# First attention: steps placed anew between the heads, and the normalised x written by ScalarE

## What is computed

```python
x = L0_attn_x                      # (32, 256, 128): 32 batches of 256 tokens of 128
xn = _layernorm(x, axis=-1)        # (x - mean) / sqrt(var + 1e-5)
x = x + _L0_attn_ref(xn, Wq, Wk, Wv, Wo) + _L0_ffn_ref(xn, ...)

# _L0_attn_ref: 16 heads of width D = 8
q, k, v = split_heads(xn @ Wq), split_heads(xn @ Wk), split_heads(xn @ Wv)
qc, kc = q - mean(q), k - mean(k)
cov = einsum('bhsd,bhtd->bhst', qc, kc) / D
scores = cov + q_var[..., :, None] * k_var[..., None, :] / D   # variances with ddof=1
out = einsum('bhst,bhtd->bhsd', softmax(scores), v)
return out.transpose(0, 2, 1, 3).reshape(b, s, e) @ Wo
```

## Time and profile before

| | us |
|---|---|
| median of 3 runs | 1303.16 |
| lowest, highest | 1302.62, 1307.37 |
| the profiled execution | 1305.62 |
| its span | 1304.0 |
| TensorE busy (matmul) | 1059.3 |
| VectorE busy | 780.4 |
| GpSimd busy | 704.3 |
| ScalarE busy | 677.1 |
| mean granted clock of TensorE | 0.838 of 2.4 GHz |

### The profile page before, as it was taken

How to read it: one execution, slowest core, us unless ns; L and a number is a source line. 1 busy time by engine, 2 the same in 40 slices (tenths; PEclk the granted TensorE clock), 3 DMA queues, 4 the chain that set the end, 5 groups by cost and what they waited for, 6 DMA issues and landing times.

```text
span 1304.0 us, 35270 instructions
## 1 busy us (share of the span) xinstructions
PE 1059.3 (81%) x12261; PEld 635.2 (49%) x12278; DVE 780.4 (60%) x2112; ACT 677.1 (52%) x1315; POOL 704.3 (54%) x1078
## 2 busy tenths in 40 slices
PE   1378878878888724999988988989888989889887
PEld 0345546555655512788844444444444444444443
DVE  3557667676675642333367667666677666766662
ACT  2155665665566211444436566556666555555565
POOL 3125565566556464222246677566686565765661
PEclk9978777777777755999969799878989877898799
DMA  7232212212212127777611111111111111111110
GB/s 153 31 99 50 48 52 63 47 47 61 54 42 51 41 35 164 219 224 221 193 41 39 31 37 39 33 29 33 41 35 36 33 29 33 37 33 33 26 43 26
DMA packets 135621, 84.23 MB, mean 65 GB/s; under 512 B 39936, under 2 KB 122752, under 8 KB 135552
## 3 DMA queue, kind: packets, MB, share of 16 engines
q1 hardware_dynamic: 124160, 55.98, 17.1%
q0 software_dynamic: 11392, 27.35, 8.1%
HBM read 49.02 MB, written 33.73 MB: 63 GB/s over the span
## 4 chain that ended last, share of the span: by engine, by line
PE 63%; ACT 11%; DVE 10%; issue 9%; SPq 3%; DMA 2%; POOL 0%; ACTq 0%; DVEq 0%; POOLq 0%
PE bank L678 53%; DVE rowmin L1144 4%; PE bank L716 3%; PE bank L772 2%; ACT Vexp L1577 2%; PE bank L956 1%; ACT oT L1490 1%; ACT h2s L1615 1%; ACT prob L1584 1%; ACT gxh L1592 1%; PE bank L778 1%; PE bank L688 1%; ACT gxb L1598 1%; DVE rsum L1162 1%; ACT oT_all L1509 1%
## 5 line engine op out<-in xcount | busy, mean ns | idle before, releaser
L1531 ACT ACTIVATE prob<-bank 128x512 f32<-128x512 f32 x512 | 302.9, 599 | 248.3 <-PE bank L678 242.7
L1144 DVE TENSOR_REDUCE rowmin<-bank 128x2 f32<-128x512 f32 x512 | 329.7, 685 | 99.0 <-PE bank L678 98.9
L678 PE MATMUL bank<-QKT 32*128 32x256 f16 x2048 | 218.6, 296 | 54.9 <-DVE rowmin L1144 50.7
L678 PE MATMUL bank<-prob,V 128*25 128x256 f32 x2048 | 157.1, 430 | 0.7 <-ACT prob L1531 0.7
L678 PEld LDWEIGHTS bank<-QKT 32*128 32x128 f16 x2048 | 63.7, 95 | 192.4 <-DVE rowmin L1144 85.2
L558 POOL DMA_INDIRECT token_rows<-rows,spots x128 | 127.6, 997 | 36.8 <-issue 36.8
L604 POOL DMA_INDIRECT xa<-expert_out,place x128 | 125.9, 984 | 39.3 <-issue 29.7
L502 POOL TENSOR_TENSOR sq<-feat 128x512 f32<-128x512 f32 x32 | 33.2, 1039 | 151.5 <-ACT feat L1502 151.5
L1666 ACT ACTIVATE hmid<-bank,wrow,up_scale 128x512 f32<-128x512 f32 x80 | 57.9, 773 | 95.0 <-PE bank L678 95.0
L678 PE MATMUL bank<-hnT,in_wT 128*128 128x512 f32 x64 | 59.8, 1033 | 52.5 <-ACT hnT L1546 36.4
L618 POOL DMA_DIRECT2D expert_out<-y x40 | 30.2, 754 | 122.3 <-DVE y L1420 118.7
(11 more groups left out here) (223 smaller groups left out, 2062.6 us busy)
## 6 DMA issues: line engine op xcount, KB each, us to landing
xrow<-token_rows SPq DMA_DIRECT2D x40, 258.0 KB, 3.2
wrow<-weight_rows SPq DMA_DIRECT2D x40, 257.0 KB, 3.4
expert_out<-y POOLq DMA_DIRECT2D x40, 256.0 KB, 3.0
token_rows<-xrow SPq DMA_DIRECT2D x16, 258.0 KB, 6.6
xg<-in_L_attn_x SPq DMA_DIRECT2D x64, 64.0 KB, 1.9
x_in<-in_L_attn_x SPq DMA_DIRECT2D x32, 128.0 KB, 2.3
xa<-in_L_attn_x SPq DMA_DIRECT2D x64, 64.0 KB, 2.0
out_base<-acc SPq DMA_DIRECT2D x64, 64.0 KB, 1.7
```

Of the source, the lines that this page charges most:

```text
L678: return pe.matmul(o, l, r, start=start, stop=stop, skip_group_check=True)
L1144: dve.tensor_reduce(rowmin[h // 8][:, :, h % TILE_ROWS, h // TILE_ROWS % HALF], row_scores[i % 3][:].rearrange("p (s t) -> p s t", s=ST), ...
L1531: act.activation(prob[:, h % 8].rearrange("p t s -> p (t s)"), col_scores[h % 2][:], ACT.Exp, scale=exp_register).then_inc(s_exp, 1)
```

## The change

The tables get new numbers: on all three engines the pieces stand at other heads, so that the groups of probability x V come at heads 2, 6, 11 and 15 instead of 1, 5, 9 and 13, and two pieces often share a head. VectorE does `split_shift(1)` and the statistics before the head's row maximum instead of behind it, and out, half0 and half1 stand at another distance from TensorE's. The normalised x is no longer written by GpSimd: VectorE makes var + eps and -mean (two operations of two columns), GpSimd makes rstd and -mean x rstd of them, and ScalarE writes xn with two ACTIVATEs (Identity, with scale and bias per partition) at head 5.

```diff
--- before.py
+++ after.py
@@ -40,10 +40,10 @@
 
 
 LEAD = 4
-PE_AT = dict(half1=0, out=3, merge=6, half0=8, project=11, v=2, shift0=7, x=10, qk=12, shift1=15)
-DVE_AT = dict(half1=0, out=2, shift0=4, half0=7, shift1=12, statistics=1)
-ACT_AT = dict(shift1=0, copy_out=2, v=3, merged=7, shift0=8, x=10, output=12, features=13)
-PE_PV = (5, 9, 13, 1)
+PE_AT = dict(half1=0, out=5, merge=7, half0=9, project=13, v=3, shift0=5, x=7, qk=9, shift1=13)
+DVE_AT = dict(half1=1, out=5, half0=10, statistics=0, shift1=12, shift0=3)
+ACT_AT = dict(shift1=0, copy_out=2, v=3, normalise=5, shift0=6, merged=7, x=7, features=9, output=14)
+PE_PV = (6, 11, 15, 2)
 
 
 
@@ -203,6 +203,9 @@
         stats = sb("stats", [P, ST, 6])
         mv = sb("mv", [P, ST, 2])
         rstd = sb("rstd", [P, ST])
+        var_x = sb("var_x", [P, ST])
+        minus_mean = sb("minus_mean", [P, ST])
+        centre = sb("centre", [P, ST])
         minus_half = sb("minus_half", [P, 2 * TILES])
         epsilon = sb("epsilon", [P, TILES])
         xn = sb("xn", [P, ST, E])
@@ -356,6 +359,7 @@
         s_x = [sem(f"s_x{p}") for p in range(2)]
 
         s_var = sem("s_var")
+        s_rstd = sem("s_rstd")
         s_xn = sem("s_xn")
         s_xt_ps = sem("s_xt_ps")
         s_xt = sem("s_xt")
@@ -478,18 +482,13 @@
                 pool.tensor_tensor(gain_root[:], gain[:], minus_half[:, 0:1], ALU.pow)
                 pool.tensor_tensor(var_scale[:], exp_scale[:], halves[:, 0:1], ALU.pow).then_inc(s_gain_root, 1)
 
-            def normalise_x(n, p):
+            def scale_x(n):
                 pool.wait_ge(s_var, n + 1)
                 if positive(n):
-                    pool.wait_ge(s_xt_ps, n)
-                pool.tensor_tensor(rstd[:], mv[:, :, 1], epsilon[:, 0:ST], ALU.add).then_inc(s_pool, 1)
+                    pool.wait_ge(s_xn, n)
+                pool.tensor_tensor(rstd[:], var_x[:], minus_half[:, 0:ST], ALU.pow).then_inc(s_pool, 1)
                 pool.wait_ge(s_pool, own.next())
-                pool.tensor_tensor(rstd[:], rstd[:], minus_half[:, 0:ST], ALU.pow).then_inc(s_pool, 1)
-                pool.wait_ge(s_pool, own.next())
-                for st in range(ST):
-                    ins = pool.tensor_scalar(xn[:, st, :], x_in[p][:, st, :], mv[:, st, 0:1],
-                                             rstd[:, st:st + 1], ALU.subtract, ALU.mult)
-                ins.then_inc(s_xn, 1)
+                pool.tensor_tensor(centre[:], minus_mean[:], rstd[:], ALU.mult).then_inc(s_rstd, 1)
 
             def features_stack(n, p):
 
@@ -623,7 +622,7 @@
                 own.count = 0
                 pool.sem_clear(s_pool)
                 if norm:
-                    normalise_x(b + 3, 1 - p)
+                    scale_x(b + 3)
                 if cur:
                     gather(b, p)
                 if norm:
@@ -1125,7 +1124,10 @@
                 dve.wait_ge(s_dve, own.next())
                 for st in range(ST):
                     ins = dve.bn_aggr(mv[:, st, :], stats[:, st, :])
-                ins.then_inc(s_var, 1)
+                ins.then_inc(s_dve, 1)
+                dve.wait_ge(s_dve, own.next())
+                dve.tensor_scalar(var_x[:], mv[:, :, 1], EPS, None, ALU.add)
+                dve.tensor_scalar(minus_mean[:], mv[:, :, 0], -1.0, None, ALU.mult).then_inc(s_var, 1)
 
 
             def half_out(n, p, k):
@@ -1440,15 +1442,16 @@
                         normalise_out(b - 1)
                     if h == DVE_AT["half0"] and prep:
                         half_out(b + 2, p, 0)
+                    if h == DVE_AT["statistics"] and norm:
+                        x_statistics(b + 3, 1 - p)
+                    if h == DVE_AT["shift1"] and nxt:
+                        split_shift(b + 1, 1)
                     rows, n, q, i = leading(b, p, h)
                     if rows:
                         take_max(n, i)
-                    if h == DVE_AT["statistics"] and norm:
-                        x_statistics(b + 3, 1 - p)
                     if h == DVE_AT["shift0"] and nxt:
                         split_shift(b + 1, 0)
-                    if h == DVE_AT["shift1"] and nxt:
-                        split_shift(b + 1, 1)
+
             def zero():
                 own.count = 0
                 dve.sem_clear(s_dve)
@@ -1488,6 +1491,15 @@
                 if positive(b):
                     act.wait_ge(s_on_ps, b)
                 act.copy(oT[:].rearrange("p u s -> p (u s)"), pv_bank[:]).then_inc(s_ot, 1)
+
+            def normalise_x(n, p):
+                act.wait_ge(s_rstd, n + 1)
+                if positive(n):
+                    act.wait_ge(s_xt_ps, n)
+                for st in range(ST):
+                    ins = act.activation(xn[:, st, :], x_in[p][:, st, :], ACT.Identity, bias=centre[:, st:st + 1],
+                                         scale=rstd[:, st:st + 1])
+                ins.then_inc(s_xn, 1)
 
             def x_out(n, p):
                 act.wait_ge(s_xt_ps, n + 1)
@@ -1675,6 +1687,8 @@
                 for h in range(H):
                     if cur:
                         probabilities(b, h)
+                    if h == ACT_AT["normalise"] and norm:
+                        normalise_x(b + 3, 1 - p)
                     if h == ACT_AT["copy_out"] and prev:
                         copy_out(b - 1)
                     if h == ACT_AT["features"] and norm:
```

## The result

The kernel with the change takes 1168.19 us, median of 4 runs (1159.20 to 1175.21); the kernel before took 1305.26 us beside it (4 runs). The ratio is 0.8934, 95% interval 0.8855 to 0.9013. The forecast was 1177 us, range 1160 to 1232.

The account below looks back on a forecast made before the run. TensorE's waits and clock falls were taken to bound batches 1 to 29; at 15.4 us each without falls they take 446.6 instead of 572.7 us, so 1303.16 - 126.1 = 1177 us, range 1160 to 1232.

Parts of the forecast that it names:

- What bounds it, and why it waits: First attention, batches 1 to 29: TensorE waits 2.57 of 17.74 us, finished rows standing behind waits in VectorE's in-order queue.
- The falls: 14 falls of TensorE's clock to 1.2 GHz in batches 1 to 29, costing 58.2 us; no more expected after the change.
- the thin stretch: From head 1's to head 5's probability x V; TensorE busy only 1.93 of its last 3.4 us, right before each fall.
- The sum of a batch: A full-clock batch: 15.17 - 0.5 + 0.2 = 14.9 us by the terms; 15.4 taken, bounds 14.8 and 17.2.
- stumbles: TensorE and VectorE, within 1.3 us of each other, hinder each other a few tenths where no earlier wait shows.
- The wait left at head 5: TensorE ahead of head 5's passes: 0.1 to 0.3 us left of 1.26, as copy_out and head 3's exponential still delay it.
- x by ScalarE: Normalised x: GpSimd loses 1.6 us, ScalarE gains 0.9, VectorE 0.2 to 0.4, at no cost while each keeps a microsecond free.
- B: Rival: clock stays up but waits return at copy_out and ahead of rstd; batch 16.6 us, 1212 us in all; chance 0.17.
- C: Rival: the clock falls as before, feared behind the transposes at heads 7 to 9; 1246 us; chance 0.13.
- D: Rival: the clock falls and doesn't come back; 1368 us if low for three quarters of the time; chance 0.05.
- E: Rival: the change does not do what it says, only x's move counts; 1303 us; chance 0.05.

Follow-up runs that it names:

- dve_only_2: The kernel before with three numbers of VectorE's table changed (out 3, half0 9, half1 1), TensorE's order untouched: 1200.91 us, ratio 0.9165.
- early_dve_2: The changed kernel with VectorE's out, half0 and half1 ahead of TensorE's again (out 4, half0 8, half1 0): 1213.58 us, ratio 0.9261.
- fill_turn: The kernel before with eight unused transposes of the identity in TensorE's 1.26 us wait ahead of head 5: 1241.31 us, ratio 0.9470.
- after_again: The changed kernel unaltered, run again as a reference: 1178.40 us, ratio 0.8996 against the kernel before.
- order_only: The kernel before with the new tables and VectorE's new order, GpSimd still writing xn: 1165.99 us, ratio 0.8887.
- x_only: The changed kernel with the old tables and VectorE's old order, ScalarE's normalise at head 8: 1317.08 us, ratio 1.0085 against the kernel before.

## Why the prediction was right, point by point

- **What bounds it, and why it waits.** Right for the wait that matters, and shown from both sides: VectorE moved behind TensorE alone brings 99.7 us (dve_only_2), VectorE moved ahead again loses 38.4 (early_dve_2). That these causes "add up to the waits in the earlier trace rows" is wrong. VectorE's place for out made the 1.26 us at head 5, and those were gone when it moved (together with half0 and half1). The waits ahead of out and of half0 are for ScalarE's copies (0.29 and 0.38 in the brackets of the earlier trace rows). The 0.36 ahead of head 0, which I put down to half1, did not change when VectorE's half1 moved behind. It went only with the whole new order, in which shift1 no longer stands right ahead of head 0 and VectorE's `split_shift` comes before a maximum; which of the two ended it, no run here separates.
- **The falls.** 58.2 us by windows, 56.8 by fill_turn. That the thin stretch causes them was argued from where they stood. Filling it ended them, and so did taking the wait out of it (dve_only_2).
- **The sum of a batch.** 14.9 by terms, and the batch without a blocked operation takes 14.92. I predicted 15.4 and 15.36 came, but not for my reason. I added 0.5 for stumbles of "a few tenths at places that no wait of before shows". Such stumbles are there, 0.27 + 0.14 us, but they are paid for inside the 14.9: with the 0.16 at head 5 the waits left are 0.57 us instead of 0.2, and in return other steps that stand together save up to a tenth each as heads do, which I had counted for passes alone, some 0.3 us in all. half0 takes 0.46 next to qk (796.67 to 797.13), half1, the same work, alone 0.55 (804.10 to 804.65). What brings the mean from 14.9 to 15.36 is the blocked operations. The agreement of 15.4 is luck.
- **The wait left at head 5.** Forecast 0.1 to 0.3. 0.16 are left there in the short batch, inside the pair at 792.38; 0.27 at head 12 and 0.14 at 789.73 came beside it, places that I hadn't walked.
- **x by ScalarE, "at no cost".** Wrong. GpSimd's and ScalarE's parts are as forecast (GpSimd is busy 11.8 us in the short batch, 11.7 were forecast; the two ACTIVATEs take 0.86 us together, with no idle ahead of them), and centre is there at 807.07, 1.8 us ahead of ScalarE's start at 808.87 (forecast 1.3). The step that failed is VectorE's: two operations of 0.17 us, "0.2 to 0.4 with the wait". One of them takes up to 0.75 in 23 of 28 batches, and the 0.6 are on TensorE's path, 14.1 us in all (16.3 in after_again). I had also called the 1.6 us off GpSimd worth nothing, since it stood idle 4.4 of 17.7 us. At 15 us a batch it has no such room; they are worth 6.8 us, as TensorE would wait for xn (order_only).
- **What else moved.** Batch 0 and the rest stayed within 2 us each, as forecast. The profiled execution's span is 1164.4 us, 13.5 less than its forecast of 1177.9, and 10.6 of them are that batch 0 began early in it. The median in after_again is 1178.4, so how near the 1177 come is in part luck too. A slip in the forecast: batches of 14.9 us give 1163 us, not 1166.
- **The rivals.** No wait came back (B) but the small ones named. The clock did not fall (C, D), the transposes at heads 7 to 9 included. That only x's move would count (E) is what x_only rules out.

## What to carry to other kernels

On an engine with a strict order, put a step that collects another engine's result behind that result, not ahead: the finished work queued behind the wait is what costs. Where the clock falls always at the same place of a loop, look for the thinnest stretch right before, and fill or close that one. Before work is shared out between VectorE and GpSimd, look at what the other does at that moment: a 0.17 us operation on SBUF can cost 0.6 on the critical path, and the same operation on GpSimd itself 0.2. And count an engine's room against the new length of the loop, not the old: GpSimd's 4.4 idle us were gone at 15.15.

## What the runs showed of the hardware

- A small VectorE operation between SBUF tensors can be held until a running GpSimd operation ends. It depends on the moment: all 15 long var_x began 0.01 to 0.10 us after an operation of L519 began; 12 others began 0.60 to 0.62 us into one, when 0.11 to 0.13 were left of it, and took 0.17. The 8 long minus_mean began 3 to 8 ns after one; in batches 8, 10, 22 and 24 it began 2 ns before to 0 ns after one, and took 0.16. Not every such operation is held: the statistics (L1122 and L1126), also between SBUF tensors and partly beside the same L519, took at most 0.29 and 0.18 us in all batches. The row maxima, which read PSUM, took 0.66 to 0.70 us whatever GpSimd did. The trace of before holds no such case (L1152 160 to 166 ns). In order_only L1152 was held by other operations of GpSimd, mostly to 0.59 us and once to 1.73. The Trainium skill (SBUF — State Buffer, SBUF: two separate sides) has a rule that fits: VectorE, for an operation in a two-port mode or with two SBUF inputs, and GpSimd share a pair of ports, and whichever starts first keeps it for its whole instruction. By that rule the held operation ends with GpSimd's, and the trace agrees (15 of 15 var_x, 8 of 8 minus_mean within 30 ns). Which of the ports it was, and whether var_x ran in such a mode, no run here shows.
- Eight f32 matmuls written plainly ran as sixteen instructions and 2.05 us, the same eight as transposes as eight and 1.10 us.
- One program took 1154 us on one chip and 1319 on another, with stands of TensorE of up to 3.5 us that the first didn't show. That was not tried further.
